# Second expert layer: slot products ahead of the products of routing weights and output biases in TensorE's order

## The reference

```
logits = xf @ Wr + br                                   # T x E
topv, _ = top_k(logits, 2)
weights = softmax(where(logits >= topv[:, 1:2], logits, -inf))
h = gelu(einsum('td,edh->eth', xf, W1) + b1[:, None, :])
expert_out = einsum('eth,ehd->etd', h, W2) + b2[:, None, :]
out = einsum('etd,te->td', expert_out, weights)
x = x + out
```

## Time and profile before

| | us |
|---|---|
| median of 3 runs | 2760.72 |
| the profiled execution's own time | 2764.75 |
| its span | 2762.5 |
| TensorE (PE) busy | 2495.7 |
| VectorE (DVE) busy | 1896.9 |
| GpSimd (POOL) busy | 1681.6 |
| ScalarE (ACT) busy | 1659.1 |

### The profile page before, as it was taken

One profiled execution on the slowest core, in us unless ns is written; L12 is line 12 of the kernel. 1 busy time (PEld: TensorE's weight loads), 2 busy tenths in 40 slices (PEclk: granted clock), 3 DMA queues, 4 the chain that ended last, 5 costly groups with the idle time before them and its releaser, 6 DMA issues. The chain is left out here.

```text
span 2762.5 us, 46203 instructions
## 1 busy us (share of the span) xinstructions
PE 2495.7 (90%) x15241; PEld 1507.9 (55%) x15242; DVE 1896.9 (69%) x3413; ACT 1659.1 (60%) x2660; POOL 1681.6 (61%) x1457
## 2 busy tenths in 40 slices
PE   4999999999999999999997599568999999779997
PEld 2455555555555555555553488534555554357886
DVE  5678767787677877677675684456888888668443
ACT  3455665556655566555554385226787878648664
POOL 3467766676757676666658444416676769834443
PEclk9999999999999999999999599879999999959998
DMA  3000000000000000000000462311111110146223
GB/s 120 20 1 1 25 1 1 1 1 1 25 1 1 1 1 1 1 1 1 1 1 23 150 193 47 82 39 42 30 42 29 44 26 23 39 139 189 46 46 66
DMA packets 82725, 103.60 MB, mean 38 GB/s; under 512 B 16225, under 2 KB 70962, under 8 KB 82546
## 3 DMA queue, kind: packets, MB, share of 16 engines
q1 hardware_dynamic: 64402, 71.55, 8.7%
q0 software_dynamic: 16288, 25.50, 5.2%
q10 hardware_dynamic: 1856, 4.19, 0.4%
HBM read 68.70 MB, written 21.64 MB: 33 GB/s over the span
## 5 line engine op out<-in xcount | busy, mean ns | idle before, releaser
L396 POOL TENSOR_TENSOR a_acc<-a_acc,a_pf 128x512 f32<-128x512 f32 (+1 forms) x480 | 644.7, 1343 | 388.0 <-ACT a_pf L524 367.8
L1935 POOL TENSOR_TENSOR c_pl<-c_pf,c_ph 128x512 f16<-128x512 f32 x320 | 378.2, 1210 | 174.2 <-ACT c_ph L2034 173.9
L524 ACT ACTIVATE a_pf<-a_psS 128x1024 f32<-128x1024 f32 (+1 forms) x288 | 281.2, 976 | 303.7 <-PE a_psS L663 303.7
L813 DVE TENSOR_TENSOR a_pl<-a_pf,a_ph 128x512 f16<-128x512 f32 x448 | 404.6, 912 | 27.5 <-ACT a_ph L530 27.5
L789 DVE TENSOR_REDUCE a_mx<-a_psA 128x1 f32<-128x512 f32 x512 | 344.5, 684 | 48.9 <-PE a_psA L600 42.7
L530 ACT ACTIVATE a_ph<-a_psS 128x1024 f16<-128x1024 f32 (+1 forms) x288 | 281.0, 976 | 0.0
L1318 POOL DMA_INDIRECT f_yd<-f_xn,f_sidx x78 | 136.6, 1752 | 231.8 <-DVE f_xn L1630 220.0
L2262 DVE TENSOR_REDUCE c_mx<-c_psA 128x1 f32<-128x512 f32 x384 | 250.8, 684 | 34.6 <-PE c_psA L2105 32.6
L2027 ACT ACTIVATE c_pf<-c_psS 128x1024 f32<-128x1024 f32 x192 | 197.7, 1030 | 89.9 <-PE c_psS L2137 89.0
L784 DVE TENSOR_TENSOR a_vl<-a_psA,a_vh 128x256 f16<-128x256 f32 (+1 forms) x272 | 115.0, 423 | 167.3 <-ACT a_vh L469 164.4
L1156 DVE TENSOR_TENSOR f_xn<-f_xn 128x256 f16<-128x256 f32 x312 | 130.0, 424 | 127.6 <-ACT f_xn L1127 120.9
(11 more groups left out here) (319 smaller groups left out, 6402.3 us busy)
## 6 DMA issues: line engine op xcount, KB each, us to landing
f_stage<-in_L_ffn_w SPq DMA_DIRECT2D x16, 1024.0 KB, 5.3
f_stage<-in_L_ffn_W SPq DMA_DIRECT2D x16, 1024.0 KB, 5.4
c_kst<-c_khs SPq DMA_DIRECT2D x64, 100.1 KB, 2.2
a_cx<-in_ctx SPq DMA_DIRECT2D x4, 1536.0 KB
c_cx<-in_ctx SPq DMA_DIRECT2D x12, 512.0 KB, 4.1
f_xrow<-f_xn SPq DMA_DIRECT2D x8, 512.0 KB, 3.1
f_yd<-X POOLq DMA_DIRECT2D x8, 512.0 KB
c_kst<-c_kls SPq DMA_DIRECT2D x32, 100.1 KB, 2.2
```

Source lines behind the costliest of these rows:

```text
L396: g.tensor_tensor(acc[0:k, p, :], acc[0:k, p, :], pf[0:k, q % RF, i, :], ALU.add).then_inc(s_acc, 1)
L524: act.activation(pf[0:r, q % RF, 0:k, :], psS[q % 2][0:r, 0:k, :], ACT.Exp, scale=SCALE).then_inc(s_pF, 1)
L813: v.tensor_tensor(pl[0:r, q % RP, i, :], pf[0:r, q % RF, i, :], ph[0:r, q % RP, i, :], ALU.subtract).then_inc(s_pL, 1)
L1935: g.tensor_tensor(pl[0:r, q % RP, i, :], pf[0:r, q % RF, i, :], ph[0:r, q % RP, i, :], ALU.subtract).then_inc(s_pG, 1)
```

## The change

In the second expert layer (`layer` is 1) TensorE's loop over the eight pairs of bias products moves behind its loop over the 32 slot products. The loops themselves, their waits, all tiles and banks, and the lists of the other engines stay as they were. Line numbers shift: the slot products are L1454 before and L1448 after, the bias products L1447 before and L1456 after.

```
                 pe.wait_ge(s_wtF, NQ)
+
+            for i in range(2 * NT):
+                q, t = i // NT, i % NT
+                pe.wait_ge(s_him, q + 1)
+                pe.wait_ge(s_lo, i // (2 * NT // NLO) + 1)
+                ins = pe.matmul(psI, olo[:, q, t, :], ohi[:, q, t, :], start=(i == 0), stop=(i == 2 * NT - 1))
+            ins.then_inc(s_id, 1)
+
+            if layer:
                 for i in range(NT // 2):
                     if i >= 3:
                         pe.wait_ge(s_wbF, i - 2)
                     for u in range(2):
                         ins = pe.matmul(psH[i % 3][:, u * D:(u + 1) * D], wt[:, 2 * i + u, :], b2[:, :], start=True, stop=True)
                     ins.then_inc(s_wbP, 1)
-
-            for i in range(2 * NT):
-                q, t = i // NT, i % NT
-                pe.wait_ge(s_him, q + 1)
-                pe.wait_ge(s_lo, i // (2 * NT // NLO) + 1)
-                ins = pe.matmul(psI, olo[:, q, t, :], ohi[:, q, t, :], start=(i == 0), stop=(i == 2 * NT - 1))
-            ins.then_inc(s_id, 1)
-
-            if layer:
                 pe.wait_ge(s_wbF, NT // 2)
                 pe.wait_ge(s_tab, 1)
             pe_turn(pe, main, 0, 0)
```

More of the change, by code:

```diff
@@ L1442, in _ @@
                 pe.wait_ge(s_wtF, NQ)
[L1443 to L1448, removed]
             for i in range(2 * NT):
@@ L1457, in _ @@
             if layer:
+                for i in range(NT // 2):
+                    if i >= 3:
+                        pe.wait_ge(s_wbF, i - 2)
+                    for u in range(2):
+                        ins = pe.matmul(psH[i % 3][:, u * D:(u + 1) * D], wt[:, 2 * i + u, :], b2[:, :], start=True, stop=True)
+                    ins.then_inc(s_wbP, 1)
                 pe.wait_ge(s_wbF, NT // 2)
```

## The result

The changed kernel takes 2763.29 us (median of 17 runs, 2761.49 to 2767.77), the kernel before 2759.11 (17 runs, 2756.38 to 2763.27). The ratio is 1.0017, its 95% interval 1.0009 to 1.0024: 4.7 us slower, between 2.5 and 6.6. I had forecast 1.5 us slower, 2762.2, and a range of 2758 to 2766. Sign and range held; the size was three times too small. That the time itself is only 1.1 off is luck: the median of 3 runs that I started from (2760.72) lies 1.6 above the median of 17.

The account below looks back on a forecast made before the run. TensorE, 90% busy, bounds the whole kernel, but the second expert layer's start waits on a chain of steps. First Gelu 4.1 us late, less what two stalls give back, leaves 1.5: 2760.72 + 1.5 = 2762.2 us, range 2758 to 2766.

Parts of the forecast that it names:

- Part one: Second expert layer's start: with the slot products first, gidx and the gather's chain come 3.2 us earlier.
- Part two: Bias products behind: last copy 13 us later, fourth add holds the low splits, first Gelu 4.1 us later (2.3 without hold).
- Part three: First chunk: two ScalarE stalls, 1.50 us at the fifth Gelu and 1.41 for expert 3's weights, absorb part of the lateness.
- The fifth Gelu's wait: First chunk on ScalarE: the 1.50 us wait for a hidden product all but goes, leaving the loop 2.6 us late.
- my reason: TensorE's products turn short 5.5 us after the first hidden product, so it is ready at 2485.2, ScalarE at 2485.1.
- the price of expert 2's weights: Loads of expert 2 issued after 2473.9 with 6.8 us left; at the median 5.6 us, no wait was counted.
- the wait for expert 3: First split of expert 3: weights land at 2491.7, ScalarE comes at 2491.4, in place of a 1.41 us wait.
- the slower rival: Weights come late beside transfers of X: +1.2 us for expert 2, +5.1 at expert 3, time 2767; chance 0.12.
- The clock: Faster rival: bias products keep TensorE busy, bringing its full clock, copies about 1.2 us apart, time 2755; chance 0.05.
- The gather alone: Rival: ScalarE's queue has slack for the bias copies, so the whole 3.2 us gain stays, time 2757.5; chance 0.07.

Follow-up runs that it names:

- e1: Changed kernel with GpSimd's fourth add held back until VectorE's eight low splits of expert 1 are done; +1.6 us against the kernel before, ratio 1.0007.
- e4: Changed kernel with each of GpSimd's transfers of X issued right behind its add; +3.3 us against the kernel before, ratio 1.0010.
- e3: Changed kernel with ScalarE's eight high splits of expert 1 ahead of its eight bias-product copies; -1.7 us against the kernel before, ratio 0.9993.
- e2: Changed kernel with GpSimd's transfers of X held back until expert 2's weights have landed; +5.7 us against the kernel before, ratio 1.0023.
- e9: Changed kernel run again, unchanged; +5.0 us against the kernel before, ratio 1.0015.
- e6: Kernel before with VectorE's copy b1e moved ahead of its low splits of expert 1; -1.0 us against the kernel before, ratio 0.9999.
- e7: e3 with the first chunk's transposes and copy xh ahead of the last three pairs of bias products; -2.0 us against the kernel before, ratio 0.9995.
- e10: Changed kernel with the edits of e3 and e4 together; -3.7 us against the kernel before, ratio 0.9988.

## Why the prediction was right, and where it was not

**Part one, the slot products first: right.** gidx 3.2 us earlier, as worked out from the first layer. The gather left the path: the transposes at 2463.81 waited for the last copy.

**Part two, the bias products behind: right in every step that counted.** GpSimd's adds began at +14.4, 1 us sooner than I had worked out, and nothing hung on it, since the fourth waits for the last copy. Copies 1.71 apart, the last at +22.3 (I had 2468.5, which is +22.1), fourth add just ahead of the low splits, low splits held, first Gelu 4.1 late. The hold is shown by the split of 2427 ns, by e1 (4.91 without the add beside it) and by e4 (two adds, 8.08). The Trainium skill's rule in "SBUF — State Buffer", "SBUF: two separate sides", is that whoever starts first blocks the other for its whole instruction. The held split of the changed kernel agrees: it started 0.47 us behind the add and ended 0.55 us after it. In e4 only the blocking agrees, not the order: by the profile one split took 3.51 us from 2466.1, though it started 0.6 us ahead of the fourth add (2466.69 to 2469.05), and it too ended only after the add. That the path went through ScalarE's queue is shown by e3.

**Part three, what the loop gives back: right but for one load.** The fifth Gelu's wait went, as said. In the changed kernel ScalarE had lost 2.92 us for expert 2 by then, so this alone doesn't bear out my reason. e2 does: the first Gelu stands at +33.57 as there, nothing waits for expert 2, and the fifth Gelu comes at +38.5 with no wait. TensorE's short products began 4.9 us after its first hidden one in e2, where I had taken 5.5; in the changed kernel it was 7.9 (2471.6 to 2479.5).

The step that failed is the price of expert 2's weights, which stood at nothing in the sum. I had the issue (2473.9 in the old count, +27.5; it was +27.8) and the 6.8 us that were left, and I let the median of 5.6 decide. The row that counted was the longest of twelve, 8.0, since it alone lay beside the transfers of X; with both loads beside them it was 9.4 and 11.4. It cost 2.9 us. Against this the wait for expert 3 went wholly, where I had left 0.3 of 1.4; its load took 5.1 us, near the 5.6 that I had put in. Forecast 4.1 - 1.5 - 1.1 = 1.5, measured in the trace 4.1 + 2.9 - 1.5 - 1.4 = 4.1, and by the runs 4.2 to 5.0. The mechanism stood in the text as the slower rival, at a chance of 0.12, priced at 1.2 us for expert 2 and a slow load of expert 3 on top, which didn't come; it was worth more than half, for nothing in the profile spoke of a load that escaped the transfers. The repeat e9 shows that it wasn't chance, e2 that the transfers caused it. The Trainium skill ("DMA: Bandwidth & Descriptors", "Queues, rings and completion order") says that each DMA engine takes turns between the queues that have work. By that, as an estimate, two streams side by side each go at half speed, and the 5.0 us of e2 would be 10; 9.4 is near it. In the trace the turns show from 2472 on. The load was issued at 2468.71, and from 2470 to 2472 it moved 0.01 MB, while GpSimd's queue had all of the engines' time (0.54 MB). From 2472 to 2478 it was 1.14 MB for SyncE's queue against 1.05 for GpSimd's.

**The rivals.** The clock: 14 us of bias products at 0.50, the copies 1.71 apart; it did not come. The rule of the Trainium skill that a busy TensorE gets its full clock ("TensorE: Matmul & The Clock Gate", Part 1) did not hold for these products: 14 us of them without a pause ran at 0.50. The gather alone: ruled out by the first Gelu.

The first split of expert 3 sums all this up: over the eleven other profiles of the table it stands as far from that of before as the medians do, within 1.7 us. e6's ratio (0.9999) shows less than its 1.6 us, but the interval (0.9990 to 1.0008) has room for it.

## What to carry to other kernels

When two groups of products change places on one engine, look for who copies the later group out and what stands behind those copies: here the products themselves did no harm, but splits of weights and the next loads were queued behind their copies, and moving these ahead (e3) took back 6 us, more than the whole loss. Where a step is delayed, price the loads that it triggers by the landing times of loads that ran beside the same traffic, not by the median. And move heavy transfers and the loads that are waited for apart together, for one alone moves the wait to the next load (e2); so does an earlier start of the loop (e7).

## What was not expected of the hardware

- b1e, eight numbers a partition, took 0.16, 0.65, 1.88, 2.00 and 4.98 us, according to which of GpSimd's adds it met. In the first profile it started beside the second of four adds, outlasted that and the third, and ended with the fourth (2474.35 against 2474.31), so back-to-back adds weren't interrupted. The copy behind it, two numbers a partition, took 5.23 us in e6 and 3.01 in e10.
- The four gathers were issued in 4.9 us (from gidx to the adds 6.1) in the changed kernel, where VectorE was idle beside them, against 6.0 (7.1 from gidx) before and 6.0 in e3, where the low splits ran beside them.
- With an idle TensorE of 1.57 us inside the first chunk, the short products began 7.9 us after the first hidden one, against 5.5 in the first layer and 4.9 in e2, both without such a pause. Before, with a pause of 3.03 us, it was 12.4 (2469.43 to 2481.8). Both profiles of the changed kernel have the pause of 1.57, e2 hasn't; why is open.
